# Passes 2 to 4 with groups 0 and 1 interleaved, the identity of pass 3 added into the matrix tiles, and pass 3's scaling moved to the scalar engine

## The chip, the cores and the metric

The kernel runs on one core of a Trainium2 chip. The time is the device time of one execution in microseconds (us); lower is better. The engines are named as in the profile: PE is TensorE (PEld its weight loads), DVE is VectorE, ACT is ScalarE, POOL is GpSimd, SP is the engine that issues the DMAs here.

## The reference

Four graph layers over 4096 nodes with 128 features and one dense 4096x4096 matrix `adj` follow one another; the second multiplies by `adj` twice.

```python
h = relu(layernorm(x)); x = x + (adj/rowsum) @ h @ W_in + (adj.T/colsum) @ h @ W_out   # layer 0
h = relu(layernorm(x)); x1 = silu(adj @ h @ W + b)                                      # layer 1
x = x + silu(adj @ x1 @ W + b)
h = relu(layernorm(x)); x = x + relu(norm(adj + I) @ h @ W + b)                         # layer 2
h = relu(layernorm(x)); x = x + relu(norm(adj + I) @ (h @ W) + b)                       # layer 3
# norm(A) = A * d[:, None] * d[None, :], d = 1/sqrt(row sums of A)
```

## The kernel before, in words

**Passes.** Layer 0 is one stage of 256 substeps, which reads `adj` and `adj_t`. Then come four passes of 128 substeps over `adj_t`: passes 1 and 2 are layer 1, pass 3 is layer 2, pass 4 is layer 3. The 4096 output nodes of a pass are 4 groups of 1024, and a group takes 32 substeps, one for each block of 128 input nodes. A substep is one tile of 128x1024 (512 KB). In layers 2 and 3 the column factor `d` is folded into the layer norm's scale (L588, L594), and the row factor `d` is applied to the finished product (L653).

**One substep.** SP issues the load of the tile into one of 14 places (`raw` and `acc`, L334). ACT copies it to `a_hi` in the rounded fp32r form (`hi`, L395), DVE takes the remainder `a_lo = tile - a_hi` (`lo`, L531), and PE multiplies six times 128x512: `a_hi` with the high and with the low part of the features, and `a_lo` with the high part (`products`, L760 and L764), summed in the two PSUM banks of the group. `a_hi` and `a_lo` have 6 places each in the passes, so ACT can start tile n only when PE has finished tile n-6. All four engines take the substeps in one fixed order, each in its own queue. "Lead" below is how long before PE starts its two `a_lo` products of a tile DVE has that tile's `a_lo` ready.

**A quarter's follow-up.** A finished group is followed up in two quarters of 512 nodes each. For each one ACT copies the bank to `prod_t` (`prod_out`, L446); PE multiplies it by the layer's weights (`finish`, L781); DVE brings the result out (`z_out`: L650 in passes 1 and 2, four L653 and one L659 in passes 3 and 4). In pass 2 ACT applies silu (L454) and DVE adds to x (L665). In passes 2 and 3 the next layer norm follows: DVE statistics (L569, L573), POOL for the root, DVE factors (`ln_affine`, L587 to L597), then ACT `ln_relu` (four L431 and L412) and DVE `split_lo` (L562), which give the high and low part of the next features. These pieces are written into the queues behind fixed substeps of the group that is running then: `AT_Z = 5` puts `z_out` behind substep 5 of the quarter's slot, statistics at 8, factors at 11, `ln_relu` at 13, `split_lo` at 14. The second quarter comes 16 substeps after the first, or 8 where the running group is group 0 of a pass (`late`, `LATER`, `LATER_FIRST`). PE waits in a pass's group 0, before every fourth block, for the features of that quarter (`h_ready`).

**Identity.** In pass 4 DVE adds the identity into the 128x128 square of the tile that holds the diagonal before ACT reads it (`plus`, L525), two substeps ahead. In pass 3 PE adds it with 16 small products of the own features with an identity matrix, once per group, behind substep 20 (`identity_product`, L822).

**Degrees.** In layer 0 DVE makes the reciprocals of row and column sums four times (`degrees`), two chains of five small dependent instructions each.

Of the kernel before, what the change touches and what calls it, by code (L numbers as in the profile page):

```python
# [11 lines left out]
P = 128  # L12
# [3 lines left out]
def build_gnn_stack(nc, x, adj, adj_t, w_in, w_out, w1, b1, w2, b2, w3, b3, out):  # L16
# [19 lines left out]
    KEPT = ((0, 30), (0, 31), (1, 30), (1, 31))  # L36

    ctx = ExitStack()
    with ctx:
# [69 lines left out]
        silu_ready = sem("silu_ready")  # L109
        x_upd = sem("x_upd")  # L110
# [47 lines left out]
        def n_of(sweep, g, s):  # L158
            return S0 + ((sweep - 1) * NG + g) * NS + s

        seq1 = []
        for k0, k1 in ((0, 2 * CB), (2 * CB, 3 * CB), (3 * CB, NB)):
            for g in range(NG - 1):
                seq1 += [(g, k, k == 0, k == NB - 1) for k in range(k0, k1)]
        seq1 += [(NG - 1, k, k == 0, k == NB - 1) for k in range(NB)]
        assert len(seq1) == NG * NS

        def last_of(sweep, g):  # L170
            return S0 + seq1.index((g, NB - 1, False, True)) if sweep == 1 else n_of(sweep, g, NS - 1)

        substeps = [(adj if kind else adj_t, d, k) for _, kind, d, k, _, _ in seq]
        substeps += [(adj_t, g, k) for g, k, _, _ in seq1]
        substeps += [(adj_t, g, k) for sweep in range(1, SWEEPS) for g in range(NG) for k in range(NB)]
# [36 lines left out]
        PLUS_AHEAD = 2  # L212
        plus_cols = {}
        plus_n = {}
        for g in range(NG):
            for b in range(CB):
                n = n_of(SWEEPS, g, g * CB + b)
                plus_n[n] = len(plus_cols)
                plus_cols[n] = slice(b * P, (b + 1) * P)
# [27 lines left out]


        LATER, LATER_FIRST = 16, 8
        AT_PROD, AT_WEIGHTS = (3, 4), (1, 3)  # L250
        AT_Z = 5
        AT_SILU = {1: 8, 2: 7}
        AT_STATS = 8
        AT_AFFINE = 11
        AT_HI = {1: 8, 2: 13, 3: 13}
        AT_LO = {1: 9, 2: 14, 3: 14}
        AT_OWN = 20
# [33 lines left out]

        SLOT1 = 7
        START1 = last_of(1, 0) + 1 - S0

        def banks_of(sweep, g):
            return side_ps[g] if sweep == 1 else out_ps[g % 2]

        def done1(at, i):
            return [q for q in range(NQ - 2) if START1 + SLOT1 * q + at == i]

# [7 lines left out]

        def halves(at, s):
            return [h for h in range(2) if at[h] == s]  # L310

        def late(at, g, s):
            return [h for h in range(2) if at + h * (LATER if g else LATER_FIRST) == s]

        def before(sweep, g):
            return (sweep, g - 1) if g else (sweep - 1, NG - 1)
# [67 lines left out]
        def _(act):  # L384
# [58 lines left out]
            def prod_out(sweep, g, half):  # L443
                act.wait_ge(sub_used, last_of(sweep, g) + 1)
# [11 lines left out]
            def first_layer(n):  # L456
# [10 lines left out]
                if n == 40:  # L467
                    act.wait_ge(ident_made, 2)
                    act.activation(ident_r[:, :], ident[:, :], ACT.Copy).then_inc(ident_made, 1)
# [7 lines left out]
            for n in range(S0):  # L477
                _, kind, d, k, _, _ = seq[n]
                hi(n, (row_part if kind else col_part)[:, k, d:d + 1])
                first_layer(n)  # L480

            for i in range(NG * NS):
                hi(S0 + i)
                first_layer(S0 + i)
                for q in done1(AT_PROD[0], i):
                    prod_out(1, q // 2, q % 2)
                for q in done1(AT_SILU[1], i):
                    silu(1, q)
                for q in done1(AT_HI[1], i):
                    split_hi(1, q)  # L490

            for sweep in range(2, SWEEPS + 1):
                for g in range(NG):
                    ps, pg = before(sweep, g)
                    for s in range(NS):
                        hi(n_of(sweep, g, s))
                        for half in halves(AT_PROD, s):
                            prod_out(ps, pg, half)
                        if ps in (1, 2):
                            for half in late(AT_SILU[ps], g, s):  # L500
                                silu(ps, 2 * pg + half)
                        if ps == 1:
                            for half in late(AT_HI[ps], g, s):
                                split_hi(ps, 2 * pg + half)
                        if ps in (2, 3):
                            for half in late(AT_HI[ps], g, s):
                                ln_relu(ps, 2 * pg + half)
# [407 lines left out]
```

## Time and profile before

| | |
|---|---|
| time, median of 3 runs | 1122.21 us (1120.19 to 1122.62) |
| profiled execution: its time | 1121.92 us |
| profiled execution: span of the instructions | 1120.1 us |
| PE / DVE / ACT busy | 1104.8 / 1047.0 / 912.6 us |
| granted TensorE clock | 1.000 |
| HBM | 364 GB/s over the span, 405.27 MB read |

The time is 1.8 us longer than the span: work around the first and last instruction. Busy time is a union of instruction spans. DVE instructions overlap by about 0.08 us at their ends, so their cost in a full queue is the distance between two starts, which is a little less than the duration in a row. The same holds for matmuls: one of 128x512 is shown with 0.39 us, and two starts are 0.227 us apart.

### The profile page before, as it was taken

Reading aid. Unit: us, or ns where it says so; the run is one execution under the profiler, and the core shown is the slowest. Engines: PE = TensorE matmul, PEld = TensorE weight load, DVE = VectorE, ACT = ScalarE, POOL = GpSimd, SP = SyncE. Lnnn points to the kernel's source line nnn. Section 1 sums busy time; section 2 is a strip of 40 time slices with the busy share of each in tenths; the row PEclk is TensorE's granted clock in tenths of the full one; section 3 lists DMA queues with packets and bytes.
Section 4 is the critical chain, followed back from the end, with each engine's and each line's share of the span. In section 5 each row is a group of like instructions: output and inputs, shape, how many; then the busy total and the mean of one; then the engine's idle time right before and its main releaser. Section 6 shows DMA issues by size and latency. Waiting matters only on the chain.

```text
span 1120.1 us, 14768 instructions
## 1 busy us (share of the span) xinstructions
PE 1104.8 (99%) x5056; PEld 914.7 (82%) x5056; DVE 1047.0 (93%) x1458; ACT 912.6 (81%) x1282; POOL 48.0 (4%) x40
## 2 busy tenths in 40 slices
PE   6999999999999999999999999999999999999998
PEld 4788888888888878888888888888888888788886
DVE  7899998999999999989898999999999999998987
ACT  7999997799788688888787888878778778877774
POOL 0000000000000000000000111121111111100000
PEclk9999999999999999999999999999999999999999
DMA  9999999999997999999999999999999999999992
GB/s 351 409 400 401 404 389 354 352 393 409 364 380 293 358 409 408 409 379 363 358 366 372 352 364 346 362 381 329 397 335 361 372 349 337 350 409 364 381 359 115
DMA packets 113836, 408.36 MB, mean 365 GB/s; under 512 B 12641, under 2 KB 13921, under 8 KB 113761
## 3 DMA queue, kind: packets, MB, share of 16 engines
q1 hardware_dynamic: 113760, 407.42, 96.1%
q8 instruction: 40, 0.66, 0.2%
q14 instruction: 36, 0.29, 0.1%
HBM read 405.27 MB, written 2.10 MB: 364 GB/s over the span
## 4 chain that ended last, share of the span: by engine, by line
PE 79%; DVE 14%; ACT 3%; issue 2%; DMA 2%; SPq 0%; ACTq 0%; DVEq 0%
PE bank L760 50%; PE bank L764 25%; DVE a_lo L531 10%; PE bank L781 3%; DMA raw<-in_adj_t_dram 2%; ACT a_hi L395 1%; ACT a_hi L397 1%; DVE stats L569 1%; DVE x_sb L633 1%; DVE h_lo L531 1%; PE bank L822 0%; DVE acc L626 0%; DVE h_lo L562 0%; PE bank L771 0%; DVE mv L573 0%
## 5 line engine op out<-in xcount | busy, mean ns | idle before, releaser
L531 DVE TENSOR_TENSOR a_lo<-raw,a_hi 128x1024 fp32r<-128x1024 f32 x560 | 657.6, 1217 | 40.8 <-ACT a_hi L395 22.5
L760 PE MATMUL bank<-a_hi,h_hi 128*128 128x512 f32 x1400 | 437.3, 394 | 8.8 <-ACT a_hi L397 8.7
L764 PE MATMUL bank<-a_lo,h_hi 128*128 128x512 f32 x1400 | 433.9, 391 | 2.3 <-DVE a_lo L531 1.7
L395 ACT ACTIVATE a_hi<-raw 128x1024 fp32r<-128x1024 f32 x368 | 376.4, 1054 | 71.2 <-PE bank L764 54.0
L760 PE MATMUL bank<-a_hi,h_lo 128*128 128x512 f32 x1400 | 432.3, 390 | 0.0
L764 PEld LDWEIGHTS bank<-a_lo,h_hi 128*128 128x128 f32 x1400 | 261.9, 188 | 63.3 <-DVE a_lo L531 9.3
L760 PEld LDWEIGHTS bank<-a_hi,h_hi 128*128 128x128 f32 x1400 | 259.3, 188 | 61.6 <-DVE h_lo L556 7.8
L760 PEld LDWEIGHTS bank<-a_hi,h_lo 128*128 128x128 f32 x1400 | 263.4, 188 | 55.4
L397 ACT ACTIVATE a_hi<-raw 128x1024 fp32r<-128x1024 f32 x192 | 201.6, 1053 | 22.9 <-PE bank L764 10.0
L531 DVE TENSOR_TENSOR a_lo<-acc,a_hi 128x1024 fp32r<-128x1024 f32 x144 | 169.8, 1217 | 10.6 <-ACT a_hi L395 9.2
L395 ACT ACTIVATE a_hi<-acc 128x1024 fp32r<-128x1024 f32 x144 | 148.7, 1055 | 28.6 <-PE bank L764 26.9
L531 DVE TENSOR_TENSOR h_lo<-raw,h_hi 128x1024 fp32r<-128x1024 f32 x64 | 76.1, 1216 | 1.7 <-ACT h_hi L397 1.5
L397 ACT ACTIVATE h_hi<-raw 128x1024 fp32r<-128x1024 f32 x64 | 67.4, 1054 | 5.7 <-DMA raw<-in_adj_t_dram 1.8
L431 ACT ACTIVATE act_raw<-x_sb,lnbias,lnscale 128x128 f32<-128x128 f32 x96 | 39.6, 483 | 32.2 <-DVE lnbias L597 32.2
L377 POOL TENSOR_TENSOR std<-mv,eps_sb 128x4 f32<-128x4 f32 x16 | 17.4, 1087 | 908.9 <-DVE mv L573 908.9
L764 PE MATMUL bank<-h_lo,h_hi 128*128 128x512 f32 x128 | 39.7, 391 | 0.0
L760 PE MATMUL bank<-h_hi 128*128 128x512 f32 x128 | 39.5, 390 | 0.0
L760 PE MATMUL bank<-h_hi,h_lo 128*128 128x512 f32 x128 | 39.4, 389 | 0.0
L781 PEld LDWEIGHTS bank<-w_sb,prod_t 128*128 128x128 f32 x280 | 36.6, 191 | 2.7
L781 PE MATMUL bank<-w_sb,prod_t 128*128 128x128 f32 x280 | 36.8, 274 | 0.0
L397 ACT ACTIVATION_READ_ACCUMULATOR a_hi<-raw 128x1 f32 x192 | 35.7, 186 | 0.0
L380 POOL TENSOR_TENSOR rstd<-std,minus_half 128x4 f32<-128x4 f32 x16 | 29.9, 1866 | 1.3
(77 smaller groups left out, 423.2 us busy)
## 6 DMA issues: line engine op xcount, KB each, us to landing
raw<-in_adj_t_dram SPq DMA_DIRECT2D x496, 512.0 KB, 6.8
acc<-in_adj_t_dram SPq DMA_DIRECT2D x144, 512.0 KB, 6.6
raw<-in_adj_dram SPq DMA_DIRECT2D x128, 512.0 KB, 7.8
out_dram<-x_sb SPq DMA_DIRECT2D x7, 256.0 KB, 7.0
x_sb<-in_x_dram SPq DMA_DIRECT2D x3, 512.0 KB, 10.9
x_sb<-in_x_dram SPq DMA_DIRECT2D x2, 256.0 KB, 3.9
out_dram<-x_sb SPq DMA_DIRECT2D x2, 128.0 KB, 1.7
w_sb<-in_L_gnn_W_dram SPq DMA_DIRECT2D x3, 64.0 KB, 8.7
```

The lines of the kernel that those rows point to most:

```text
L377: pool.tensor_tensor(std[:, :], mv[:, :, 1], eps_sb[:, :].to_broadcast([P, GB]), ALU.add)\
L380: pool.tensor_tensor(rstd[:, :], std[:, :], minus_half[:, :].to_broadcast([P, GB]), ALU.pow)\
L395: act.activation(sub_hi_of(n), sub_raw(n), ACT.Copy).then_inc(sub_hi, 1)
L397: act.activation(sub_hi_of(n), sub_raw(n), ACT.Copy, accum_out=accum).then_inc(sub_hi, 1)
L431: last = act.activation(act_raw[:, b * D:(b + 1) * D], x_sb[:, GB * q + b, :], ACT.Relu, bias=lnbias[:, b:b + 1], scale=lnscale[:, b:b + 1])
L531: dve.tensor_tensor(sub_lo_of(n), sub_raw(n), sub_hi_of(n).bitcast(F32), ALU.subtract).then_inc(sub_lo, 1)
L569: last = dve.bn_stats(stats[:, b, :], x_sb[:, GB * q + b, :])
L633: last = dve.scalar_tensor_tensor(out=x_sb[:, block0 + b, :], in0=z_ps[half][:, b * D:(b + 1) * D], scalar=inv[:, which, half * GB + b:hal ...
L760: pe.matmul(bank[half][:, :], weights, hi_a[:, half * GW:(half + 1) * GW], start=start and weights is hi_w, stop=False)
L764: last = pe.matmul(bank[half][:, :], hi_w, lo_a[:, half * GW:(half + 1) * GW], start=False, stop=stop)
L781: last = pe.matmul(z_ps[half][:, b * D:(b + 1) * D], src[:, b * P:(b + 1) * P], w_sb[:, w, :], start=True, stop=True)
```

## The change

Five things change.

1. **Order of groups** in passes 2 to 4: group 0 blocks 0 to 23, group 1 blocks 0 to 23, group 0 blocks 24 to 31, group 1 blocks 24 to 31, then group 2 and group 3. Three pairs of PSUM banks take turns over the groups (`pair_of`) where there were two.
2. **Places of the follow-up** are now substeps counted from the end of group 0 (substep 55 of a pass): quarters in passes 2 and 3 come every 14 substeps, in pass 4 every 10; pass 1 keeps its 7, its last two come at 0 and 10 of pass 2. The last quarters of passes 2 and 3 fall into the next pass. In passes 2 and 3 `ln_relu` is behind substep 15 of a slot and `split_lo` behind 16 (before 13 and 14); silu stays at 7, statistics at 8, factors at 11.
3. **Identity** in pass 3 as in pass 4: `plus` for 64 tiles in all, now 5 substeps ahead; `identity_product` and its matrix `ident_r` are gone.
4. **Scaling of pass 3**: ACT multiplies the product by `d` in four instructions (`scale_z`, behind substep 5), and DVE adds the bias in one instruction behind substep 6, where four DVE instructions did both.
5. **Degrees**: row and column sums in one array, one chain of five instructions each time.

```diff
+        for sweep in (2, 3, 4):
+            order[sweep] = [(0, 0, 3 * CB), (1, 0, 3 * CB), (0, 3 * CB, NB), (1, 3 * CB, NB), (2, 0, NB), (3, 0, NB)]
...
+        for sweep in (2, 3, 4):
+            for g in range(NG):
+                pair_of[sweep, g] = (sweep - 2 + g) % 3
...
-        PLUS_AHEAD = 2
+        PLUS_AHEAD = 5
...
+        for n, (sweep, g, k) in enumerate(passes, S0):
+            if sweep >= 3 and k // CB == g:
...
-        LATER, LATER_FIRST = 16, 8
...
-        AT_HI = {1: 8, 2: 13, 3: 13}
-        AT_LO = {1: 9, 2: 14, 3: 14}
-        AT_OWN = 20
+            slot[1, q] = n_of[1, 0, NB - 1] + 1 + 7 * q if q < NQ - 2 else n_of[2, 0, 0] + 10 * (q - NQ + 2)
+            for sweep in (2, 3):
+                slot[sweep, q] = n_of[sweep, 0, NB - 1] + 1 + 14 * q
+            if q < NQ - 2:
+                slot[4, q] = n_of[4, 0, NB - 1] + 1 + 10 * q
...
+        PASS_WEIGHTS = places({1: 1, 2: 1, 3: 1, 4: 1})
+        PASS_PROD = places({1: 3, 2: 3, 3: 3, 4: 3})
+        PASS_Z = places({1: 5, 2: 5, 3: 6, 4: 5})
+        PASS_SILU = places({1: 8, 2: 7})
+        PASS_SCALE = places({3: 5})
+        PASS_STATS = places({2: 8, 3: 8})
+        PASS_AFFINE = places({2: 11, 3: 11})
+        PASS_HI = places({1: 8, 2: 15, 3: 15})
+        PASS_LO = places({1: 9, 2: 16, 3: 16})
...
+            def scale_z(sweep, q):
+                act.wait_ge(z_ready, z_of(sweep, q) + 1)
+                act.wait_ge(x_upd, (sweep - 2) * NQ + q)
+                if q == 0:
+                    act.wait_ge(dsq_ready, 3)
+                for b in range(GB):
+                    last = act.activation(zt[:, b * D:(b + 1) * D], z_ps[q % 2][:, b * D:(b + 1) * D], ACT.Copy,
+                                          scale=d_isqrt[:, GB * q + b:GB * q + b + 1])
+                last.then_inc(scaled_ready, 1)
...
-                inverse_degree(inv[:, 0, :], row_part[:, CB * b:CB * b + CB, :])
-                inverse_degree(inv[:, 1, :], col_part[:, CB * b:CB * b + CB, :])
+                link(dve.tensor_reduce(deg[:, 0, :, :], deg_part[:, :, CB * b:CB * b + CB, :], AX_X, ALU.add))
...
+                elif sweep == 3:
+                    dve.wait_ge(scaled_ready, q + 1)
+                    bias = b_sb[:, B_OF[sweep]:B_OF[sweep] + 1, :].to_broadcast([P, GB, D])
+                    ins = dve.tensor_tensor(zt4, zt4, bias, ALU.add)
...
-            def identity_product(sweep, g, bank):
-                src = SET_OF[sweep - 1]
-                for half in range(2):
-                    for b in range(GB):
-                        for part in (h_hi[src], h_lo[src]):
-                            pe.matmul(bank[half][:, b * P:(b + 1) * P], part[:, CB * g + GB * half + b, :], ident_r[:, :],
-                                      start=False, stop=False, skip_group_check=True)
```

How the orders change is shown at three places. First ACT's queue over one quarter of pass 2, before; L395 is the copy of a tile, L446 the bank copy, L454 silu, L431 and L412 `ln_relu`.

```order
255 L395 ACTIVATE a_hi<-raw 128x1024 x3
256 L454 ACTIVATE zt<-zt 128x512
257 L395 ACTIVATE a_hi<-raw 128x1024 x6
258 L431 ACTIVATE act_raw<-x_sb,lnbias,lnscale 128x128 x4
259 L412 ACTIVATE h_hi<-act_raw 128x512
```

The same of the changed kernel, where L391, L460, L427 and L408 are these instructions.

```order
262 L391 ACTIVATE a_hi<-raw 128x1024 x4
263 L460 ACTIVATE zt<-zt 128x512
264 L391 ACTIVATE a_hi<-acc 128x1024 x4
265 L391 ACTIVATE a_hi<-raw 128x1024 x4
266 L427 ACTIVATE act_raw<-x_sb,lnbias,lnscale 128x128 x4
267 L408 ACTIVATE h_hi<-act_raw 128x512
```

Between silu and `ln_relu` stand 8 tile copies now, and 6 before.

Second, DVE's queue over the second quarter of pass 3: before, L653 and L659 are `z_out`, L569 and L573 the statistics, and L587 is the first of the five factor instructions.

```order
508 L531 TENSOR_TENSOR a_lo<-raw,a_hi 128x1024 x2
509 L653 SCALAR_TENSOR_TENSOR zt<-bank,d_isqrt,b_sb 128x128 x4
510 L659 SCALAR_TENSOR_TENSOR x_sb<-zt,x_sb 128x512
511 L531 TENSOR_TENSOR a_lo<-raw,a_hi 128x1024 x3
512 L569 BN_STATS stats<-x_sb 128x6 x4
513 L573 BN_AGGR mv<-stats 128x2 x4
514 L531 TENSOR_TENSOR a_lo<-raw,a_hi 128x1024 x3
515 L587 TENSOR_TENSOR newton<-rstd 128x4
```

The same quarter of the changed kernel; L524 is the subtraction, L518 the identity add.

```order
518 L518 TENSOR_TENSOR raw<-raw,ident 128x128
519 L524 TENSOR_TENSOR a_lo<-acc,a_hi 128x1024
520 L643 TENSOR_TENSOR zt<-zt,b_sb 128x512
521 L652 SCALAR_TENSOR_TENSOR x_sb<-zt,x_sb 128x512
522 L518 TENSOR_TENSOR raw<-raw,ident 128x128
523 L524 TENSOR_TENSOR a_lo<-acc,a_hi 128x1024
524 L518 TENSOR_TENSOR raw<-raw,ident 128x128
525 L524 TENSOR_TENSOR a_lo<-acc,a_hi 128x1024
526 L562 BN_STATS stats<-x_sb 128x6 x4
527 L566 BN_AGGR mv<-stats 128x2 x4
```

The four scaling instructions became one addition, and an identity add stands ahead of each of 8 successive subtractions.

Third, PE's queue in pass 3 before, where the identity product begins behind a group's substep 20; the changed kernel has no such rows.

```order
1629 L760 MATMUL bank<-a_hi,h_hi 128x512 x2
1630 L760 MATMUL bank<-a_hi,h_lo 128x512 x2
1631 L764 MATMUL bank<-a_lo,h_hi 128x512 x2
1632 L822 MATMUL bank<-ident_r,h_hi 128x128
1633 L822 MATMUL bank<-ident_r,h_lo 128x128
```

Sixteen of the L822 rows stand there for each group; 64 are gone from PE.

## Rows read from the trace of the kernel before

**Rows 1.** The page, part 1: busy us, share of span, instructions.

```profile
PE 1104.8 (99%) x5056; PEld 914.7 (82%) x5056; DVE 1047.0 (93%) x1458; ACT 912.6 (81%) x1282; POOL 48.0 (4%) x40
```

**Rows 2.** Waits of PE and PEld, 730 to 970 us: total, times, longest.

```profile
PE bank L764 <- DVE a_lo L531: 1.1, 2, 0.7
PEld bank L764 <- DVE a_lo L531: 4.1, 7, 1.1
```

**Rows 3.** Timeline of PE, 766 to 777 us: start, length, instruction, idle before.

```profile
766.19 0.61 PE L760 MATMUL bank<-a_hi,h_lo 128*128 128x512 f32 x2
767.46 0.73 PE L764 MATMUL bank<-a_lo,h_hi 128*128 128x512 f32 x2 [0.65 <-DVE a_lo L531]
...
770.32 0.62 PE L764 MATMUL bank<-a_lo,h_hi 128*128 128x512 f32 x2
...
771.68 0.62 PE L764 MATMUL bank<-a_lo,h_hi 128*128 128x512 f32 x2
772.13 0.22 PE L822 MATMUL bank<-ident_r,h_hi 128*128 128x128 f32 x1
...
774.87 0.62 PE L764 MATMUL bank<-a_lo,h_hi 128*128 128x512 f32 x2
```

**Rows 4.** Timeline of PE, 521 to 524 us, around a weight product.

```profile
521.57 0.62 PE L764 MATMUL bank<-a_lo,h_hi 128*128 128x512 f32 x2
...
523.84 0.39 PE L764 MATMUL bank<-a_lo,h_hi 128*128 128x512 f32 x1
```

**Rows 5.** Timeline of DVE, 700 to 724 us: one quarter of pass 2.

```profile
700.74 0.68 DVE L650 TENSOR_TENSOR zt<-bank,b_sb 128x512 f32<-128x512 f32 x1
...
704.74 0.68 DVE L665 TENSOR_TENSOR x_sb<-zt,x_sb 128x512 f32<-128x512 f32 x1
...
706.67 1.19 DVE L531 TENSOR_TENSOR a_lo<-raw,a_hi 128x1024 fp32r<-128x1024 f32 x1
...
710.05 0.15 DVE L587 TENSOR_TENSOR newton<-rstd 128x4 f32<-128x4 f32 x1
...
710.71 2.35 DVE L531 TENSOR_TENSOR a_lo<-acc,a_hi 128x1024 fp32r<-128x1024 f32 x2
714.12 1.22 DVE L531 TENSOR_TENSOR a_lo<-raw,a_hi 128x1024 fp32r<-128x1024 f32 x1 [1.06 <-ACT a_hi L395]
715.26 0.68 DVE L562 TENSOR_TENSOR h_lo<-act_raw,h_hi 128x512 fp32r<-128x512 f32 x1
715.86 8.03 DVE L531 TENSOR_TENSOR a_lo<-raw,a_hi 128x1024 fp32r<-128x1024 f32 x7
723.81 0.68 DVE L650 TENSOR_TENSOR zt<-bank,b_sb 128x512 f32<-128x512 f32 x1
```

**Rows 6.** Timeline of ACT over the same quarter.

```profile
710.82 1.65 ACT L431 ACTIVATE act_raw<-x_sb,lnbias,lnscale 128x128 f32<-128x128 f32 x4 [2.06 <-DVE lnbias L597]
...
713.04 9.59 ACT L395 ACTIVATE a_hi<-raw 128x1024 fp32r<-128x1024 f32 x10
```

**Rows 7.** Timeline of DVE, 795 to 840 us: z_out of pass 3.

```profile
816.80 1.11 DVE L653 SCALAR_TENSOR_TENSOR zt<-bank,d_isqrt,b_sb 128x128 f32<-128x128 f32 x4
...
818.56 3.49 DVE L531 TENSOR_TENSOR a_lo<-raw,a_hi 128x1024 fp32r<-128x1024 f32 x3
```

**Rows 8.** Timeline of DVE, 927 to 936 us: an identity add of pass 4.

```profile
928.07 0.28 DVE L525 TENSOR_TENSOR raw<-raw,ident 128x128 f32<-128x128 f32 x1
928.27 1.22 DVE L531 TENSOR_TENSOR a_lo<-raw,a_hi 128x1024 fp32r<-128x1024 f32 x1
```

**Rows 9.** Timeline of DVE, 176 to 232 us: the first degrees.

```profile
176.97 0.18 DVE L608 TENSOR_REDUCE deg<-row_part 128x8 f32<-128x32 f32 x1
...
179.10 2.36 DVE L531 TENSOR_TENSOR a_lo<-raw,a_hi 128x1024 fp32r<-128x1024 f32 x2
```

**Rows 10.** Waits of PEld, 170 to 235 us, then 395 to 410 us.

```profile
PEld bank L764 <- DVE a_lo L531: 1.1, 3, 0.5
...
PEld bank L764 <- DVE a_lo L531: 1.4, 2, 1.1
```

**Rows 11.** DMA issues by line: KB each, median us from issue to landing.

```profile
raw<-in_adj_t_dram SPq DMA_DIRECT2D x496, 512.0 KB, 6.8
```

More of the change, by code:

```diff
@@ L109, in build_gnn_stack @@
         silu_ready = sem("silu_ready")
+        scaled_ready = sem("scaled_ready")
         x_upd = sem("x_upd")
@@ L289, in build_gnn_stack @@
         FIRST_LO = {0: 1, 2: 2, 4: 3, 27: 4, 43: 5, 59: 6, 72: 7, 85: 8, 98: 9}
-        SLOT1 = 7
-        START1 = last_of(1, 0) + 1 - S0
         def banks_of(sweep, g):
-            return side_ps[g] if sweep == 1 else out_ps[g % 2]
-        def done1(at, i):
-            return [q for q in range(NQ - 2) if START1 + SLOT1 * q + at == i]
+            return run_ps[pair_of[sweep, g]]
         LOAD_X = {11: 2, 36: 3, 62: 4}
@@ L478, in _ @@
                 _, kind, d, k, _, _ = seq[n]
-                hi(n, (row_part if kind else col_part)[:, k, d:d + 1])
+                hi(n, deg_part[:, 1 - kind, k, d:d + 1])
                 first_layer(n)
[L482 to L507, printed above, removed]
+            for n in range(S0, len(substeps)):
+                hi(n)
+                first_layer(n)
+                if n in PASS_PROD:
+                    sweep, q = PASS_PROD[n]
+                    prod_out(sweep, q // 2, q % 2)
+                if n in PASS_SILU:
+                    silu(*PASS_SILU[n])
+                if n in PASS_SCALE:
+                    scale_z(*PASS_SCALE[n])
+                if n in PASS_HI:
+                    sweep, q = PASS_HI[n]
+                    if sweep == 1:
+                        split_hi(sweep, q)
+                    else:
+                        ln_relu(sweep, q)
             act.wait_ge(tail_ready, 1)
             act.wait_ge(z_ready, z_of(SWEEPS, NQ - 2) - 1)
-            act.activation(prod_t[:, 0, :], out_ps[(NG - 1) % 2][0][:, :], ACT.Copy).then_inc(prod_ready, 1)
+            act.activation(prod_t[:, 0, :], banks_of(SWEEPS, NG - 1)[0][:, :], ACT.Copy).then_inc(prod_ready, 1)
             act.wait_ge(tail_ready, 2)
@@ L837, in _ @@
                 first_layer(n)
-            pe.wait_ge(ident_made, 3)
-            for i, (g, k, first, last) in enumerate(seq1):
-                if first and g < NG - 1:
-                    pe.wait_ge(part_added, drained(len(runs) - 3 + g)[1])
-                elif first:
-                    pe.wait_ge(prod_ready, prod_of(1, 1) + 1)
-                if g == 0 and k % GB == 0:
-                    pe.wait_ge(h_ready, split_n(0, k // GB) + 1)
-                products(S0 + i, h_hi[1][:, k, :], h_lo[1][:, k, :], banks_of(1, g), first, last)
-                first_layer(S0 + i)
-                for q in done1(AT_WEIGHTS[0], i):
-                    finish(1, q // 2, q % 2)
@@ L852, in _ @@
-            for sweep in range(2, SWEEPS + 1):
-                hi_set, lo_set = h_hi[SET_OF[sweep - 1]], h_lo[SET_OF[sweep - 1]]
-                for g in range(NG):
-                    ps, pg = before(sweep, g)
-                    bank = out_ps[g % 2]
-                    pe.wait_ge(prod_ready, prod_of(sweep, 2 * g) - 2)
-                    for s in range(NS):
-                        if g == 0 and s % GB == 0:
-                            pe.wait_ge(h_ready, split_n(sweep - 1, s // GB) + 1)
-                        if sweep == SWEEPS and g == NG - 1 and s >= NS - TAIL:
-                            continue
-                        products(n_of(sweep, g, s), hi_set[:, s, :], lo_set[:, s, :], bank, s == 0, s == NS - 1)
-                        if sweep == 3 and s == AT_OWN:
-                            identity_product(sweep, g, bank)
-                        for half in halves(AT_WEIGHTS, s):
-                            finish(ps, pg, half)
+            for n in range(S0, len(substeps) - TAIL):
+                sweep, g, k = passes[n - S0]
+                src = SET_OF[sweep - 1]
+                if k == 0:
+                    if bank_before[sweep, g] is None:
+                        pe.wait_ge(part_added, drained(len(runs) - 3 + g)[1])
+                    else:
+                        bs, bg = bank_before[sweep, g]
+                        pe.wait_ge(prod_ready, prod_of(bs, 2 * bg + 1) + 1)
+                if g == 0 and k % GB == 0:
+                    pe.wait_ge(h_ready, split_n(sweep - 1, k // GB) + 1)
+                products(n, h_hi[src][:, k, :], h_lo[src][:, k, :], banks_of(sweep, g), k == 0, k == NB - 1)
+                first_layer(n)
+                if n in PASS_WEIGHTS:
+                    sweep, q = PASS_WEIGHTS[n]
+                    finish(sweep, q // 2, q % 2)
```

122 lines of the change are left out of this document (49 added, 73 removed).

## The prediction

> **What bounds the kernel now.** I read the busy times first: PE 99%, DVE 93% [rows 1]. A busy PE could still be one that is fed late, so I looked next at how evenly it runs. Two `a_lo` products of neighbouring substeps start 1.36 us apart, 770.32 and 771.68 [rows 3]; 512 substeps of the passes at that pace are 696 us, and nearly all the rest of PE's time there is weight products. A weight product makes the distance 523.84 - 521.57 = 2.27, so it costs 0.91 us [rows 4]. PE is the bound, and a saving counts only if it shortens PE's own list or one of its waits. The view of waits shows few: in passes 2 to 4 PEld waits seven times for DVE's `a_lo`, 4.1 us, PE itself 1.1 us [rows 2]. One of them: 766.19 to 767.46 where 0.45 is normal, a loss of 0.82 [rows 3]. Over the seven I take 3.3 us, between 1.1 and 4.1.
>
> Why DVE is late is in its timeline over a quarter of pass 2 [rows 5]. A subtraction costs 7.95/7 = 1.136 us in a full queue (715.86 to 723.81), so against PE's 1.36 DVE gains 0.22 us per substep. The quarter's own work is `z_out` 0.60, x plus silu and statistics 1.93 (704.74 to 706.67), factors 0.66 (710.05 to 710.71) and `split_lo` 0.60: 3.8 us. And DVE stands idle for 1.06 us before the subtraction at 714.12. The cause is ACT's queue [rows 6]: `ln_relu` waits for the factors, takes 713.04 - 710.82 = 2.2 us, and only then comes the next tile copy, while DVE had two tiles (2.3 us) in hand. From quarter to quarter DVE needs 23.07 us (700.74 to 723.81), PE 16 x 1.36 + 0.91 = 22.67. DVE loses 0.4 us of lead per quarter from a lead that cannot pass about 5 us (six places: five substeps and 0.9 less ACT's and DVE's own time for a tile), and the waits are where it is used up.
>
> **Part by part.** The sum is made against the profiled execution, 1121.9 us, 0.3 below the median of the runs.
>
> *Identity off PE.* From 771.68 to 774.87 are 3.19 us, 1.83 more than a substep [rows 3]. Four groups: -7.3 us, all on PE's list, so sure. The Trainium skill's page "VectorE: DVE Perf Modes", section on the TRN2 errata, gives a matmul max(60, 6+N) cycles at 2.4 GHz. By it these 64 of 128 columns would cost 3.6 us in all, and the sum would come out 3.7 us worse; the row shows 1.83 per 16, and the row decides.
>
> *Identity onto DVE in pass 3.* An add costs 928.27 - 928.07 = 0.20 us [rows 8]; 32 more are 6.4 us of DVE, in bursts of 8 substeps in which DVE gains 0.02 instead of 0.22. ACT needs the add done; five ahead takes away waits of that sort. DVE now asks for tile n+5 before it works on n: its load was issued after subtraction n-9, nine substeps (10 us) earlier, against 6.8 us to landing [rows 11]. It holds, so nothing.
>
> *`ln_relu` two substeps later.* DVE has now four subtractions behind the factors (4.5 us) where ACT needs 2.2 plus a copy of 1.05. ACT must have copied tile +15 before the factors come; the six places allow that when PE is at +10, and DVE in trouble is just when PE has come as far as DVE has. So the idle 1.06 goes, at all 16 quarters. If it stayed, it would cost 16 x 1.06 of DVE time.
>
> *Spacing of 14.* PE gives 14 x 1.36 + 0.91 = 19.95 us per quarter, DVE needs 14 x 1.136 + 3.8 = 19.7 us. Balanced without the idle, short by 0.8 us per quarter with it. Hence the waits of passes 2 to 4 lose their cause: -3.3 us.
>
> *Scaling on ACT.* DVE's `z_out` of pass 3 took 1.76 us (816.80 to 818.56) [rows 7]; now one add (0.60 and 0.13 until its dependent can start) and one update 0.60 make 1.33, and with 1.20 of statistics, factors and `split_lo` pass 3's quarter is 3.8 us as well. The price is a new chain: PE's product, ACT's four instructions, tile copy +6, DVE. No row has this instruction. Bounds: nothing, and the 1.65 us of four `ln_relu` instructions of the same width [rows 6]; they are nearest, with one operand more, so I take 1.4. By the Trainium skill, page "ScalarE: Activation LUTs", section "What ACT_TABLE_LOAD costs", each pointer operand adds 93 ns, so four would take some 1.3 us, an estimate; the sum would gain a few tenths. ACT itself has room: 81% busy [rows 1]. The product is ready three substeps before PE starts +5; scaling 1.4, copy 1.05, subtraction 1.2 end 3.7 us after it, and PE's `a_lo` part of +6 starts 4 x 1.36 + 0.91 = 6.35 after it. So DVE's lead at +6 is cut to about 2.6 us in every quarter of pass 3. From there: -1.33 for `z_out`, -1.20 for statistics, -0.66 for factors, +0.22 a substep: the lowest point is about 0.7. That holds without an identity burst.
>
> *New waits in the bursts.* Group by group the bursts in DVE's queue begin, counted from pass 3's start, at substep -5, 27, 75, 115, and for pass 4's first groups at 123 and 155; quarters of pass 3 have their slots at 56 + 14q. Walking the lead through these: the second quarter (slot 70) loses another 1.2 us of gain before the factors, PE waits 0.5. The fifth (slot 112) lies under two bursts end to end, 16 substeps: 1.3. The sixth starts with a lead below 1: 1.0. The eighth (slot 154) lies under the burst at 155: 1.1. In pass 2 the lead starts at 5, a quarter's lowest point is near 2, and only the eighth, under the burst at 27 after one at -5, runs out: 0.8. Together +4.7; bounds 0 (the leads a few tenths better each, or a burst that falls into idle time) and about 10 (twice that).
>
> *Degrees.* A double chain takes 2.13 us (176.97 to 179.10) [rows 9]; a single one half, so -1.05 of DVE at each of four places. At two of them PE waits for DVE afterwards: at 402 us, 1.4 us of PEld waits, where 1.0 goes; at 182 to 215, 1.1 us, where I take 0.5 [rows 10].
>
> *Groups 0 and 1 side by side, three pairs of banks.* No instruction is added. The features of the last quarters are due at substep 52 of the next pass and made at 43; group 0's banks are free long before their next group. Nothing, also for SP, whose loads keep their number and spacing.
>
> Sum: -7.3 - 3.3 - 1.0 - 0.5 + 4.7 = -7.4, so 1121.9 - 7.4 = 1114.5 in the profile's terms and 1114.8 against the median; I write 1114.7.
>
> **Rivals.** *No new waits.* If the lead stays positive in the bursts, the time is 1121.9 - 12.1, about 1110. For it: my walk goes below nothing by 0.5 to 1.3 only. Against: four different quarters do.
>
> *More waits in pass 3, still no loss.* If scaling takes ACT over 2 us or a tile is late for an add, every quarter of pass 3 dips to zero and the bursts add more: 8 x 0.4 and 2 more, about 1120.
>
> *Slower.* The idle of 1.06 us before `split_lo` stays, because ACT is held at copy +15 and `ln_relu` again ends after DVE has run dry. Then each of the 16 quarters is 0.8 short, 12.8 us, and the time is about 1114.7 + 12.8 = 1127.5. It decides once the idle left per quarter passes some 0.7 us: up to 0.25 is covered by the balance above, and (0.7 - 0.25) x 16 is the gain of 7.4. For it: ACT waited 2.06 us for the factors before [rows 6], so the two queues are closely tied, and a later `ln_relu` also makes `split_lo` later. Against: four subtractions are 4.5 us against 3.3 of ACT.
>
> **How the numbers follow.** Forecast (1111.5 to 1118): 0.55. No or few new waits (below 1111.5): 0.22. More waits (1118 to 1122): 0.14. Slower: 0.09. The range 1109.5 to 1119.5 takes in the first two and half of the third. A measurement of this kernel tells 0.2%, 2.2 us, from no change. Faster than 1120 by these cases 0.85, within 0.2% 0.06, slower 0.09.
>
> **What the profile of the changed kernel would show.** PE has 64 instructions fewer and no identity rows; its busy time falls by about 7 us. No idle of 1.06 before the subtraction ahead of `split_lo`. In pass 3, once per quarter, DVE waits 1 to 3 us for ACT at substep +6, with ACT waiting for PE's product ahead of the scaling. PE's waits for `a_lo` move from the pass boundaries into the bursts, some 5 us in all, mostly in the last 40 substeps before pass 4 and the first 45 of it. Around 402 us they are gone. Wrong would be: PE waits of over 10 us in passes 2 to 4, waits for the features (`h_ready`), or ACT waiting for DMA behind 560 us.

## The result and the profile after

The changed kernel takes 1112.64 us (median of 6 runs, 1112.21 to 1113.35), the kernel before in the same runs 1121.28 us. The ratio is 0.9926 with a 95% interval of 0.9916 to 0.9935: 0.74% faster, clear of the 0.2% that a measurement tells. The profiled executions have spans of 1111.0 and 1120.1 us, 9.1 us apart.

The page of the changed kernel, part 1 (busy us, share, instructions), to be held against [rows 1]:

```profile
PE 1094.9 (99%) x4992; PEld 906.8 (82%) x4992; DVE 1045.2 (94%) x1446; ACT 922.8 (83%) x1313; POOL 48.8 (4%) x40
```

PE has 64 instructions fewer and 9.9 us less busy time. DVE's busy time is the same within 2 us: the adds went in, the scaling and the second degree chain went out. PE is still at 99%.

The waits of PE and PEld for DVE, 560 to 1100 us (passes 2 to 4), answer to [rows 2]:

```profile
PE bank L746 <- DVE a_lo L524: 1.7, 5, 0.6
PEld bank L746 <- DVE a_lo L524: 4.4, 7, 1.0
```

The total is as before, 4.4 against 4.1 us, but these are other waits: none is left in passes 2 to 4 before 850 us, and all seven lie in or just behind the bursts. The last, in PE's timeline (start, length, instruction, idle before), is at 973 us:

```profile
972.11 0.62 PE L742 MATMUL bank<-a_hi,h_lo 128*128 128x512 f32 x2
973.33 0.73 PE L746 MATMUL bank<-a_lo,h_hi 128*128 128x512 f32 x2 [0.60 <-DVE a_lo L524]
```

Between the starts are 1.22 us where 0.45 is normal. Summed in this way over the bursts PE loses 0.45 us near 854, 1.04 near 910 to 916, 0.80 near 929 to 932 and 0.87 near 973, each with 0.1 to 0.2 for a slow second matmul: 3.2 us (the expectations below write 3.1). The same sum in the kernel before gives 3.3 us, at 738, 766, 956 and 963 to 966 us. The waits are thus as dear as they were; they have only moved.

DVE over a quarter of pass 2, to be held against [rows 5]:

```profile
704.81 3.46 DVE L524 TENSOR_TENSOR a_lo<-acc,a_hi 128x1024 fp32r<-128x1024 f32 x3
...
708.85 4.62 DVE L524 TENSOR_TENSOR a_lo<-raw,a_hi 128x1024 fp32r<-128x1024 f32 x4
713.68 1.23 DVE L524 TENSOR_TENSOR a_lo<-raw,a_hi 128x1024 fp32r<-128x1024 f32 x1 [0.20 <-ACT a_hi L391]
714.82 0.68 DVE L555 TENSOR_TENSOR h_lo<-act_raw,h_hi 128x512 fp32r<-128x512 f32 x1
```

Four subtractions stand behind the factors, and the idle ahead of the last of them, just before `split_lo`, is 0.20 us in this quarter. In the 16 quarters of passes 2 and 3 together this idle is 1.0 us, in three quarters of pass 2. In the kernel before it was 1.06 us in 13 of the 16.

The new chain at the first quarter of pass 3, first ACT, then DVE:

```profile
816.35 0.60 ACT L442 ACTIVATE prod_t<-bank 128x512 f32<-128x512 f32 x1 [1.60 <-PE bank L746]
...
819.97 1.14 ACT L450 ACTIVATE zt<-bank,d_isqrt 128x128 f32<-128x128 f32 x4 [1.12 <-PE bank L763]
```

```profile
817.93 2.36 DVE L524 TENSOR_TENSOR a_lo<-raw,a_hi 128x1024 fp32r<-128x1024 f32 x2 [1.28 <-ACT a_hi L391]
822.09 1.22 DVE L524 TENSOR_TENSOR a_lo<-acc,a_hi 128x1024 fp32r<-128x1024 f32 x1 [1.80 <-ACT a_hi L391]
```

ACT waits for PE's product, scales in 1.14 us, and DVE stands idle for 1.80 us until the next tile copy. The first idle, 1.28, is the bank copy's. This quarter is the only one with such a wait: from 823 to 1000 us DVE is never idle for more than 0.1 us.

The degrees, to be held against [rows 9]:

```profile
177.19 0.21 DVE L602 TENSOR_REDUCE deg<-deg_part 128x16 f32<-128x64 f32 x1
...
178.35 2.36 DVE L524 TENSOR_TENSOR a_lo<-raw,a_hi 128x1024 fp32r<-128x1024 f32 x2
```

A chain takes 1.16 us in place of 2.13. From 395 to 410 us PE waits for nothing any more (1.4 us of PEld waits before, [rows 10]), and from 170 to 235 us 0.2 us of PEld waits are left.

### The profile page after: what moved, and what is told of

The parts are those of the page before. It is cut to its first block, busy times and chain, and to the rows that moved or that the text cites. A ratio compares the mean times of both kernels' runs of the same rounds, so it can differ in the third digit from the quotient of the medians.

```text
span 1111.0 us, 14666 instructions
## 1 busy us (share of the span) xinstructions
PE 1094.9 (99%) x4992; PEld 906.8 (82%) x4992; DVE 1045.2 (94%) x1446; ACT 922.8 (83%) x1313; POOL 48.8 (4%) x40
## 4 chain that ended last, share of the span: by engine, by line
PE 81%; DVE 15%; DMA 2%; ACT 1%; issue 1%; SPq 0%; ACTq 0%
PE bank L742 51%; PE bank L746 26%; DVE a_lo L524 11%; PE bank L763 3%; DMA raw<-in_adj_t_dram 2%; ACT a_hi L393 1%; DVE stats L562 1%; DVE x_sb L652 0%; DVE zt L643 0%; DVE raw L518 0%; DVE h_lo L555 0%; PE bank L753 0%; ACT act_raw L417 0%; DVE mv L566 0%; DVE h_lo L524 0%
## 5 line engine op out<-in xcount | busy, mean ns | idle before, releaser
L524 DVE TENSOR_TENSOR a_lo<-raw,a_hi 128x1024 fp32r<-128x1024 f32 x560 | 656.8, 1218 | 32.4 <-ACT a_hi L391 14.1
L391 ACT ACTIVATE a_hi<-raw 128x1024 fp32r<-128x1024 f32 x368 | 379.4, 1056 | 73.5 <-PE bank L746 64.8
L524 DVE TENSOR_TENSOR a_lo<-acc,a_hi 128x1024 fp32r<-128x1024 f32 x144 | 170.6, 1216 | 6.0 <-ACT a_hi L391 4.4
L391 ACT ACTIVATE a_hi<-acc 128x1024 fp32r<-128x1024 f32 x144 | 147.6, 1060 | 23.8 <-PE bank L746 22.5
L524 DVE TENSOR_TENSOR h_lo<-raw,h_hi 128x1024 fp32r<-128x1024 f32 x64 | 76.2, 1218 | 1.7 <-ACT h_hi L393 1.5
L427 ACT ACTIVATE act_raw<-x_sb,lnbias,lnscale 128x128 f32<-128x128 f32 x96 | 39.5, 482 | 12.3 <-DVE lnbias L590 12.3
```

The lines of the kernel that those rows point to most:

```text
L391: act.activation(sub_hi_of(n), sub_raw(n), ACT.Copy).then_inc(sub_hi, 1)
L427: last = act.activation(act_raw[:, b * D:(b + 1) * D], x_sb[:, GB * q + b, :], ACT.Relu, bias=lnbias[:, b:b + 1], scale=lnscale[:, b:b + 1])
L524: dve.tensor_tensor(sub_lo_of(n), sub_raw(n), sub_hi_of(n).bitcast(F32), ALU.subtract).then_inc(sub_lo, 1)
```

## The experiments

The theory to be tested: PE's own list plus DVE's lead. PE is shortened by what leaves its list; DVE costs time exactly where its work and its idle time per quarter exceed PE's, after the lead is used up. Rivals were set against it case by case. Ratios are against the kernel before in the same runs; "over the changed kernel" is the difference to 1112.6 us.

Differences of 1 or 2 us are hard to tell in the time alone, because the first substeps vary: PE reaches the same product near 160 us up to 1.9 us earlier or later from one profiled execution to another. So one stretch of the profiled executions is compared as well, from the start of PE's first `a_lo` product of pass 2 to that of its last of pass 4. It takes 554.71 us in the kernel before and 547.43 us in the changed one (557.75 to 1105.19), and 547.45 us in the kernel with two degree chains, whose passes 2 to 4 are the same as the changed kernel's. The table rests on one execution of each kernel.

| kernel | stretch of passes 2 to 4, us over the changed kernel |
|---|---|
| ln_relu back at 13 | +18.0 |
| identity of pass 3 back on PE | +4.4 |
| scaling of pass 3 back on DVE | +4.2 |
| no identity in pass 3 | -2.0 |
| groups one after the other | +0.6 |
| identity adds on POOL | +2.6 |
| quarters 15 apart | +1.5 |
| two degree chains | 0.0 |
| adds 2 ahead | +2.7 |
| scaling two substeps later | -0.6 |
| scaling later, `ln_relu` of pass 3 later, last quarters 15 apart | -1.2 |
| one part alone in the kernel before | +5.1 over the kernel before |

**ln_relu back at 13.**

```diff
-        PASS_HI = places({1: 8, 2: 15, 3: 15})
+        PASS_HI = places({1: 8, 2: 13, 3: 13})
-        PASS_LO = places({1: 9, 2: 16, 3: 16})
+        PASS_LO = places({1: 9, 2: 14, 3: 14})
```

> The changed kernel with ln_relu and split_lo of passes 2 and 3 back behind substeps 13 and 14 of a slot (from 15 and 16), nothing else. Lead theory: DVE's idle of 1.06 us per quarter comes back, a quarter needs 20.75 us of DVE against PE's 19.95, so 0.8 us is lost at each of 16 quarters, 12.8 in all, of which some 2 to 3 us are covered by the lead of 2 us left at the low points of pass 2: about 1122 us, between 1120 and 1126. Rival (the place of ln_relu doesn't matter, because PE's list is what got shorter): 1112 to 1114.

Measured 1128.81 us, ratio 1.0063 (1.0046 to 1.0080): the two substeps are worth 16 us, and without them the change is slower than the kernel before. The rival is out. DVE's waits from 560 to 1100 us:

```profile
DVE a_lo L524 <- ACT a_hi L391: 23.8, 23, 1.9
DVE zt L646 <- PE bank L763: 3.2, 3, 1.1
DVE newton L580 <- POOL rstd L376: 2.4, 2, 1.2
```

In the changed kernel the first row reads 9.6 us in 10 waits, and the one for POOL isn't there: 14.2 + 2.4 = 16.6 us more idle. The time is 16.2 us longer, and the profiled executions, from which these waits are, are 17.2 us apart. One such idle in DVE's timeline:

```profile
948.98 2.35 DVE L524 TENSOR_TENSOR a_lo<-raw,a_hi 128x1024 fp32r<-128x1024 f32 x2
952.40 1.23 DVE L524 TENSOR_TENSOR a_lo<-raw,a_hi 128x1024 fp32r<-128x1024 f32 x1 [1.06 <-ACT a_hi L391]
```

I had expected 9.4 us, and the time lies above the range of 1120 to 1126. The idle counted almost whole, and two waits for POOL came on top. That it counted whole because the lead of pass 3 is already spent in the changed kernel fits the lead there, but was not tested by itself.

**Identity of pass 3 back on PE.**

```diff
-            if sweep >= 3 and k // CB == g:
+            if sweep == 4 and k // CB == g:
...
+                if sweep == 3 and k == 20:
+                    identity_product(sweep, g, banks_of(sweep, g))
```

> The changed kernel with pass 3's identity back on PE as 16 small products per group behind its block 20, and no identity adds by DVE in pass 3. Lead theory: PE's list is 7.3 us longer, the waits of the bursts in pass 3 (3.1 us) go: about 1116.8 us (1116 to 1118). Rival (the waits come from the scaling chain through ACT, not from the adds): they stay, 1119.5 to 1120.5.

Measured 1116.20 us, ratio 0.9955 (0.9940 to 0.9970), 3.6 over the changed kernel. PEld's waits from 560 to 1100 us fall to one:

```profile
PEld bank L750 <- DVE a_lo L528: 0.7, 1, 0.7
```

So the waits of the changed kernel come with the adds, and the scaling chain, which is still there, doesn't make them by itself. PE's list is 7.3 us longer and its waits cost 2.7 us less (0.5 against 3.2), which makes 4.6; the stretch of passes 2 to 4 is 4.4 us longer.

**Scaling of pass 3 back on DVE.**

```diff
-        PASS_Z = places({1: 5, 2: 5, 3: 6, 4: 5})
-        PASS_SCALE = places({3: 5})
+        PASS_Z = places({1: 5, 2: 5, 3: 5, 4: 5})
+        PASS_SCALE = {}
```

> The changed kernel with the scaling of pass 3 back on DVE behind substep 5, nothing on ACT. Lead theory: DVE has 0.43 us more per quarter of pass 3, 3.4 us in all, but the lead is not cut to 2.8 us at the first quarters, which gives some 2 back: 1113 to 1115 us. Rival (the chain product, ACT, DVE is what lets the lead run out): the waits of 3.1 us go, 1109.5 to 1111.

Measured 1116.14 us, ratio 0.9954 (0.9939 to 0.9969), 3.5 over. PEld waits 9.0 us in 11 waits. Both numbers missed: the scaling costs the whole 3.4 us of DVE time, nothing came back from the larger lead at the start, and DVE waited 2.4 us for POOL. The rival, that the chain is the cause of the waits, is out: without the chain they more than doubled.

**No identity in pass 3.** This kernel leaves out the addition of I in layer 2.

```diff
-            if sweep >= 3 and k // CB == g:
+            if sweep == 4 and k // CB == g:
```

> The changed kernel without any identity in pass 3: the addition of I in layer 2 is left out. It is the ceiling of what the bursts of adds cost. Lead theory: the waits of 3.1 us go and nothing else: about 1109.5 us. Rival (DVE's load doesn't matter there): 1112 to 1113.

Measured 1109.89 us, ratio 0.9901 (0.9886 to 0.9916), 2.7 under the changed kernel. PEld waits 2.0 us in 3 waits, all in pass 4, just behind its own first two bursts (near 929 and 969 us). So pass 3's adds cost 2.7 us altogether. The kernel with the products on PE takes 6.3 us more than this one; PE's waits cost 0.9 us less there, so the products themselves cost the 7.2 or 7.3 that the row gave.

**One part alone in the kernel before.**

```diff
-        PLUS_AHEAD = 2
+        PLUS_AHEAD = 5
-        for g in range(NG):
-            for b in range(CB):
-                n = n_of(SWEEPS, g, g * CB + b)
+        for sweep in (3, 4):
+            for g in range(NG):
+                for b in range(CB):
+                    n = n_of(sweep, g, g * CB + b)
...
-                        if sweep == 3 and s == AT_OWN:
-                            identity_product(sweep, g, bank)
```

> The kernel before with one part of the change: pass 3's identity added by DVE, 5 substeps ahead, and the 64 products off PE. Lead theory: PE's list is 7.3 us shorter, but a quarter of pass 3 needs 24.3 us of DVE (16 subtractions, 4.2 of its own work, 1.06 idle, 0.8 of adds) against 22.67 of PE, 1.6 us short at each of 8, so some 12 us of waits are added: 1121 to 1127. Rival (the move pays by itself, as PE is the bound): 1114 to 1117.

Measured 1127.14 us, ratio 1.0053 (1.0038 to 1.0068): 7.3 us taken off the engine that is 99% busy, and the kernel is 5.7 us slower. The waits of PEld for DVE from 560 to 1100 us are 17.4 us in 28, PE's own 5.0 in 11, and DVE stood idle for ACT 23.2 us in 25 waits (25.6 in 27 in the kernel before, where the same idle did little harm). The balance per quarter foresaw it: the time is at the upper end of 1121 to 1127.

**Groups one after the other.**

```diff
-            order[sweep] = [(0, 0, 3 * CB), (1, 0, 3 * CB), (0, 3 * CB, NB), (1, 3 * CB, NB), (2, 0, NB), (3, 0, NB)]
+            order[sweep] = [(g, 0, NB) for g in range(NG)]
-                slot[sweep, q] = n_of[sweep, 0, NB - 1] + 1 + 14 * q
+                slot[sweep, q] = n_of[sweep, 0, NB - 1] + 1 + (16 * q if q < NQ - 2 else 96 + 8 * (q - NQ + 2))
-                slot[4, q] = n_of[4, 0, NB - 1] + 1 + 10 * q
+                slot[4, q] = n_of[4, 0, NB - 1] + 1 + 16 * q
```

> The changed kernel with the groups of passes 2 to 4 one after the other again: quarters in passes 2 and 3 every 16 substeps, the last two 8 apart in the next pass, quarters of pass 4 every 16. Everything else stays. Lead theory: a quarter has 22.67 us of PE against 22.0 of DVE, so the lead holds within a pass, and the last two quarters of pass 3, 8 substeps apart and behind 16 substeps of identity adds, cost 3 to 5 us of waits: 1112 to 1115. Rival (the side-by-side order is what brings the gain): 1117 or more.

Measured 1112.52 us, ratio 0.9924 (0.9909 to 0.9939). The largest part of the diff, the side-by-side order with the close quarters that it allows, is worth nothing in the time and 0.6 us in passes 2 to 4. The three pairs of banks are still there, so this run says nothing of them. PEld waits 4.6 us in 5. The largest, 1.9 us near 916, is in the sixth quarter of pass 3, under two bursts end to end, where DVE also waited 1.18 us for POOL. The next, 1.2 us near 947, is where pass 3's last two quarters come 8 apart. One of 0.8 us near 763 is where pass 2's last two do.

**Identity adds on POOL.**

```diff
+            for at in range(S0, len(substeps)):
+                if at + PLUS_AHEAD in plus_cols:
+                    m = at + PLUS_AHEAD
+                    block = sub_raw(m)[:, plus_cols[m]]
+                    pool.wait_ge(tile_in[raw_place[m]], landed[m])
+                    pool.tensor_tensor(block, block, ident[:, :], ALU.add).then_inc(plus_ready, 1)
...
-                if n + PLUS_AHEAD in plus_cols:
-                    plus(n + PLUS_AHEAD)
```

> The changed kernel with all 64 identity adds on POOL, in its queue at the same places. Lead theory: 12.8 us less on DVE, the burst waits of 3.1 us go: about 1109.5. Rival: POOL is too slow for it (its 128x4 adds took 1.1 us each, and a layer norm holds its queue for 3 us) and ACT waits for it, or DVE slows beside it: 1113 to 1125.

Measured 1114.14 us, ratio 0.9938 (0.9923 to 0.9953), 1.5 over; the rival held, in its second half. ACT did wait for POOL's adds, 7.5 us in 2, but DVE's idle for ACT stayed as it was (9.4 us in 10, against 9.6 in 10), so that wait made DVE no later. Groups of instructions from 560 to 1100 us (count, busy, mean ns, idle before):

```profile
L529 DVE TENSOR_TENSOR a_lo<-raw,a_hi 128x1024 fp32r<-128x1024 f32 x270 | 323.3, 1251 | 9.6 <-ACT a_hi L398 6.2
L375 POOL TENSOR_TENSOR raw<-raw,ident 128x128 f32<-128x128 f32 x48 | 48.7, 1036 | 102.9 <-DMA raw<-in_adj_t_dram 102.8
```

The same subtraction has a mean of 1218 ns in the changed kernel. 33 ns more over 270, and 21 ns over the 108 from `acc` (1236 against 1215), are 11 us of DVE: about what the 64 adds of 0.20 had cost (12.8).

**Quarters 15 apart.**

```diff
-                slot[sweep, q] = n_of[sweep, 0, NB - 1] + 1 + 14 * q
+                slot[sweep, q] = n_of[sweep, 0, NB - 1] + 1 + 15 * q
```

> The changed kernel with the quarters of passes 2 and 3 every 15 substeps instead of 14. Lead theory: DVE gains 0.22 us more per quarter, and the waits of 3.1 us shrink by about half: 1110.5 to 1112. Rival (late features hold up the next pass, since the last quarter ends at its substep 49 of 52): over 1113.

Measured 1113.71 us, ratio 0.9930 (0.9914 to 0.9947), not told apart from the changed kernel by the time; the stretch of passes 2 to 4 is 1.5 us longer. The rival's number held, but not its reason: PE never waited for features. Neither theory had named what the trace shows. DVE waited three times 1.18 us for POOL. One of them, DVE's timeline and then POOL's:

```profile
849.13 0.38 DVE L566 BATCH_NORM_AGGREGATE mv<-stats 128x2 f32<-128x6 f32 x4
849.42 0.26 DVE L518 TENSOR_TENSOR raw<-raw,ident 128x128 f32<-128x128 f32 x1
...
854.67 0.17 DVE L580 TENSOR_TENSOR newton<-rstd 128x4 f32<-128x4 f32 x1 [1.18 <-POOL rstd L376]
```

```profile
849.59 3.96 POOL L373 TENSOR_TENSOR std<-mv,eps_sb 128x4 f32<-128x4 f32 x1 [18.78 <-DVE mv L566]
853.63 1.01 POOL L376 TENSOR_TENSOR rstd<-std,minus_half 128x4 f32<-128x4 f32 x1
```

POOL's add took 3.96 us where 1.09 is its median. With a burst over the statistics the five factor instructions come 1.18 us late, and PE's next wait for `a_lo`, at 856.61 us, is 1.27 us; the changed kernel's in this place was 0.17.

**Two degree chains.**

```diff
-                link(dve.tensor_reduce(deg[:, 0, :, :], deg_part[:, :, CB * b:CB * b + CB, :], AX_X, ALU.add))
+                for i in range(2):
+                    link(dve.tensor_reduce(deg[:, 0, i, :], deg_part[:, i, CB * b:CB * b + CB, :], AX_X, ALU.add))
...
```

> The changed kernel with two chains of five instructions per degrees again, nothing else. Theory: 1.05 us more of DVE at each of four places, of which PE waits for two: the waits near 215 us and at 402 us of the kernel before come back, 1.5 to 2 us: 1114 to 1114.8 us. Rival (small DVE work in the first layer is hidden): within 0.5 us of the changed kernel's 1112.6.

Measured 1114.87 us, ratio 0.9940 (0.9928 to 0.9953), 2.2 over. PEld's waits from 395 to 410 us are back as they were before:

```profile
PEld bank L747 <- DVE a_lo L524: 1.4, 2, 1.1
```

and from 170 to 235 us 1.7 us are back. The two intervals overlap, but the traces are clear: from 160 us to the start of pass 2 this kernel needs 2.1 us more, and nothing more behind that. Twenty instructions of 0.17 to 0.2 us in a layer that looked uninvolved are a quarter of the gain.

**Adds 2 ahead.**

```diff
-        PLUS_AHEAD = 5
+        PLUS_AHEAD = 2
```

> The changed kernel with the identity adds 2 substeps ahead instead of 5. Theory: ACT may then be only two tiles ahead of DVE in a burst, and where a burst lies over ln_relu (2.2 us, then a copy of 1.05) DVE has only 2.7 us of work in hand: 0.6 us of idle at two or three quarters, 1113 to 1114.5 us. Rival (the distance is of no account, since ACT has time): 1112.6.

Measured 1114.66 us, ratio 0.9942 (0.9930 to 0.9955), 2.0 over. The size is near the theory's, the way is another one. Part of it is that ACT waits for adds (15.2 us in 25 waits for `raw`, none in the changed kernel), is late with what follows, and PE then waits for `prod_t`. Another part is again POOL: its add took 3.96 us at 847.20, DVE waited 1.18 us for it and made the next identity add late. The first row is ACT's wait for that add, the second PE's waits for `prod_t` over the whole span:

```profile
853.32 1.06 ACT L391 ACTIVATE a_hi<-raw 128x1024 fp32r<-128x1024 f32 x1 [2.20 <-DVE raw L518]
```

```profile
PE bank L763 <- ACT prod_t L442: 2.1, 2, 1.0
```

**Scaling two substeps later.**

```diff
-        PASS_Z = places({1: 5, 2: 5, 3: 6, 4: 5})
-        PASS_SCALE = places({3: 5})
+        PASS_Z = places({1: 5, 2: 5, 3: 8, 4: 5})
+        PASS_SCALE = places({3: 7})
```

> The changed kernel with pass 3's scaling on ACT behind substep 7 (from 5) and DVE's bias add behind substep 8 (from 6), just ahead of the statistics. Lead theory: ACT no longer waits for PE's product ahead of copy +6, so DVE's lead is not cut to 2.7 us at the first two quarters of pass 3 (its waits of 1.3 and 1.8 us for ACT go), and some 1.5 to 2 of the 3.1 us of PE waits in the bursts go: 1110.6 to 1111.3 us. Rival (the waits are made inside each burst, whatever the lead was before): 1112.6.

Measured 1111.50 us, ratio 0.9918 (0.9904 to 0.9932), the lowest of the full kernels, but its interval overlaps the changed kernel's; in passes 2 to 4 the gain is 0.6 us. PEld's waits are 3.4 us in 4 (4.4 in 7). The two waits of 1.3 and 1.8 us that the expectation puts at two quarters are both in the first one: the 1.8 shrank to 0.2, and the 1.3 is the bank copy's and stayed. The wait near 854 us is gone, those near 929 and 970 are longer. Most of what the extra lead saves is thus lost again at the later bursts. The rival describes more than half of it.

**Scaling later, ln_relu of pass 3 later, and its last quarters 15 apart.** Beside the edit of the kernel above:

```diff
-        PASS_AFFINE = places({2: 11, 3: 11})
+        PASS_AFFINE = places({2: 11, 3: 12})
-        PASS_HI = places({1: 8, 2: 15, 3: 15})
+        PASS_HI = places({1: 8, 2: 15, 3: 16})
-        PASS_LO = places({1: 9, 2: 16, 3: 16})
+        PASS_LO = places({1: 9, 2: 16, 3: 17})
-                slot[sweep, q] = n_of[sweep, 0, NB - 1] + 1 + 14 * q
+                slot[sweep, q] = n_of[sweep, 0, NB - 1] + 1 + 14 * q + (max(0, q - 3) if sweep == 3 else 0)
```

> The kernel with scaling behind 7 and the add behind 8, and in pass 3 also: factors, ln_relu and split_lo one substep later (12, 16, 17), so that four subtractions stand between the statistics and the factors that wait for POOL, and the last four quarters 15 substeps apart instead of 14. Lead theory: four quarters gain 0.22 us each and no wait for POOL can arise; 0.5 to 1.5 us of the waits left go: 1110 to 1111 us, against 1112.6 of the changed kernel. Rival (one burst's waits only move to the next): as with the scaling later alone, 1111.5.

Measured 1112.26 us, ratio 0.9925 (0.9911 to 0.9938). PEld waits 2.8 us in 4, the fewest of a kernel with all adds on DVE, but the time is not told from the changed kernel's. No wait for POOL is left, but the changed kernel had none either. Of the 2.1 us between 1108.9 us of span here and 1111.0 of the changed kernel, 0.9 lie before 160 us, in substeps that are the same in both, and 1.2 in passes 2 to 4. So the trace shows a small gain, of a size that the times can't confirm.

## Why the prediction was right

The forecast was 1114.7 us (1109.5 to 1119.5), the measured time is 1112.6. In the terms of the profiled executions: -7.4 forecast, -9.1 measured. The parts of the -9.1 can be read off PE's timeline: 0.2 us lost before 160 us, 2.1 us gained from there to pass 2 by the degrees, and 7.3 us in passes 2 to 4, where the products are gone and 3.2 us of new waits stand for 3.3 of old ones.

*What bounds.* PE's list plus a few waits for DVE, and a lead that is used up: this reading gave the way of seven of the twelve experiments, among them that the move of the identity by itself would make the kernel slower, and the kernel in order is in its range. It missed the size twice (`ln_relu` at 13, scaling on DVE). Two came out the other way: adds on POOL and quarters 15 apart should have gained and did not. In both traces POOL and DVE are in each other's way, for which the reading has no term. The last two, which should have gained 1 to 2 us, show 0.6 and 1.2 in the trace and can't be told from no gain in the time.

*Identity off PE, -7.3.* Its share agrees: with the products back passes 2 to 4 are 4.4 us longer, while 2.7 us of waits vanish, so 7.1. By the formula of the Trainium skill's page "VectorE: DVE Perf Modes" (section on the TRN2 errata), 3.6 us for the 64 products as an estimate, the step would have gained next to nothing over the waits that it brings; the measurement decides for the row.

*Idle of 1.06 and the spacing of 14, -3.3.* The waits at 738, 766, 956 and 963 us are gone, 3.3 us. The case against this step, the "slower" rival, is what the kernel with `ln_relu` back at 13 does: 1128.8 us, where 1127.5 stood. The condition on which it hung, that ACT gets to copy +15 in time, held but for 1.0 us in three quarters of pass 2. The cause was told too simply, though. Three of the four places lie at substeps 17 to 23 of a pass, where the last two quarters of the pass before came 8 substeps apart. With that spacing kept and `ln_relu` late, the kernel in order still has the waits near 763 and 947 us. So part of the 3.3 us went by the even spacing and not by the idle, which the prediction does not separate.

*Scaling on ACT.* Assumed 1.4 us, measured 1.14 in the timeline, so the estimate of 1.3 worked out from the Trainium skill's page "ScalarE: Activation LUTs" (section "What ACT_TABLE_LOAD costs") was nearer than the 1.4 taken below the row's bound. The lead at +6 of the first quarter was cut to 2.8 us (2.6 forecast). But the sign "once per quarter DVE waits 1 to 3 us for ACT" came in the first quarter alone. From the second on the bursts and the quarter's own work kept the lead at +6 at 2.8 us or less, and the chain had nothing to cut. The walk was near the right leads there, for a reason that held once. That DVE's saving is real is shown by the kernel with the scaling on DVE, +3.5 us.

*New waits, +4.7.* Measured 3.2: the step that was mis-sized. All four quarters of pass 3 that were named (slots 70, 112, 126 and 154) have their wait: 0.45, 1.04, 0.80 and 0.87 against 0.5, 1.3, 1.0 and 1.1. The fifth, at the eighth quarter of pass 2 (0.8), did not come. The lead there stayed above nothing: at its lowest DVE has the `a_lo` ready at 788.14 us and PE starts on it at 788.50. My walk was about 1.1 us too low over two bursts. There was luck in the waits that did come as well: at the two statistics under a burst POOL's add took 1.29 us, while in six of the experiments one or more such adds took 3.8 to 4.0 and held DVE up by 1.18 us. The prediction had no term for it.

*Degrees, -1.5.* Measured 2.1 in the trace: putting the chains back gives 2.2 us in the time. The waits near 215 us went almost whole, not by half, and they were more than the 1.1 us counted: the same view has a second row, 0.7 us in 2 waits for DVE's `h_lo`. Of the 1.8 us 0.2 are left.

*Side by side, nothing.* Shown for the order by the kernel in order, 1112.5. The third pair of banks was not tested.

The two misses of size point the same way: 1.5 us less of new waits and 0.6 more from the degrees. With the 0.2 lost before 160 us they make, to within 0.2, the 1.7 us between -7.4 and -9.1.

## What to carry to other kernels

When the bound engine is fed by another that is 93% busy, price a change per period of the schedule: work plus idle of the feeder against the list of the bound engine. Work moved from the first to the second is a gain only if that balance stays positive, and 1 us of idle per period, made by the order of two instructions on a third engine, can turn the sign. Small dependent instructions on the feeder count wherever its lead is spent, in stages far from the change too. Where kernels share the rest, compare the stretch of the traces that the change touches: here it repeated to 0.02 us, while the whole differed by up to 1.9 us in its first part.

## What the runs showed of the hardware

A POOL add on 128x4 values takes 1.09 us by its median, and it took 3.76 to 3.97 us ten times in six of the experiments. In all 224 cases of the 14 traces it ended 0.06 us behind the end of a DVE instruction with two SBUF inputs. Where the subtraction of 1.22 us had started 0.16 us ahead of it, it took 1.09 us; behind a `split_lo` of 0.66 us it took 0.55 (kernel in order, twice). Behind an identity add it came through with the end of the first subtraction, as here in the changed kernel (DVE, then POOL), or only with the third, as in the rows of the kernel with quarters 15 apart. The third is the last one before DVE stops to wait for POOL. What decides between the two isn't shown.

```profile
848.50 0.26 DVE L518 TENSOR_TENSOR raw<-raw,ident 128x128 f32<-128x128 f32 x1
848.67 1.22 DVE L524 TENSOR_TENSOR a_lo<-acc,a_hi 128x1024 fp32r<-128x1024 f32 x1
848.66 1.29 POOL L373 TENSOR_TENSOR std<-mv,eps_sb 128x4 f32<-128x4 f32 x1 [17.44 <-DVE mv L566]
```

In the other direction DVE's subtraction rose from 1218 to 1251 ns in the mean while POOL did the adds. The Trainium skill's page "SBUF — State Buffer", section "SBUF: two separate sides", says that VectorE and GpSimd share a port pair as an exclusive lock, also where VectorE has two SBUF inputs and GpSimd reads SBUF. The ends of POOL's adds agree with it. The lock itself was not isolated in a run of its own, and it would explain a wait for one DVE instruction, not one for three in a row.

PE's first pair of matmuls after a wait is slower: at 973.33 us the pair spans 0.73 us where 0.62 is usual, so many short waits cost PE 0.11 us each beyond the wait.
